# Indirect row writes of the last two chunks wait for the pair two back instead of the pair just in front

## The chip, the cores and the metric

The kernel is one program on one core of a Trainium2 chip, one launch. The metric is the device time of that core in microseconds (us). The engines are PE (TensorE, the matmul engine), DVE (VectorE), ACT (ScalarE), POOL (GpSimd) and SP (SyncE, which here only issues DMAs).

## What is computed

Two transformer layers over x of shape (16, 256, 128), 4096 tokens of 128 numbers, in float32. Around each half-layer stand a layer norm, a scale and a shift, and a gate. Layer 0 has causal attention and then a mixture of experts; layer 1 has a gated recurrence with a feed-forward block and then a channel mixer. The change lies in the mixture of experts of layer 0:

```python
def _L0_ffn_ref(x, gate_w, bias, up_w, up_b, down_w, down_b, sw_up, sb_up, sw_down, sb_down):
    scores = sigmoid(xf @ gate_w + bias)                      # 4096 tokens, 8 experts
    top_scores, top_idx = top_k(scores, 2)
    top_scores = top_scores / (sum(top_scores) + 1e-06)
    w = zeros((T, 8)).at[arange(T)[:, None], top_idx].add(top_scores)
    eo = gelu(up_w[e] @ x + up_b[e]) @ down_w[e] + down_b[e]  # for each expert e
    combined = einsum('teh,te->th', eo * 0.1, w)
    shared = (gelu(xf @ sw_up + sb_up) @ sw_down + sb_down) * 0.1
    out = shared + combined
    return out / (max(abs(out), axis=-1) + 1e-06)
```

Each token goes to two of the eight experts.

## The kernel before

The 4096 tokens are eight chunks of 512 (c = 0 to 7), two sequences each, and a chunk has four parts (k = 0 to 3) of 128 tokens. For each chunk the router's scores give, for every token, the two rows that it gets in the DRAM tensor `expert_rows` (`XD` in the code), where each expert has a region of its own; the row numbers stand in the tile IU (the function `dpd`, its last instruction is L1504). The chunk's tokens are transposed back into rows and copied by ACT into one of two tiles HT (`hta`, L1911; the profile calls the tile `five`). Then POOL writes them to DRAM: `scatter(c, k)` issues a pair of indirect DMAs (L2069), one for the first expert's row of each of the 128 tokens and one for the second's, 64 KB each. A pair counts on one of two semaphores, `scattered[k % 2]`, so parts 0 and 2 count on the first, parts 1 and 3 on the second; each pair adds 32, and a chunk adds 64 to each. Ahead of its pair each `scatter` waits for the pair just in front to have landed (L2067).

The experts work on tiles of 256 rows, 39 in all (the last ones have 128). The first 17 (N1) hold only rows of chunks 0 to 5 and can start before chunks 6 and 7 are written; every later tile waits for all eight chunks. For a tile t:

- `fetch(t)` on SP reads the expert's weights WE (L2187, 512 KB), the bias BD (L2188) and the tile's rows XT (L2191, 128 KB). It needs the output of tile t − 6 to be done, as there are six buffers, and from tile 17 on XT's read also waits for all scatters (L2190).
- `xt` on PE transposes XT (L1149), and `xs` on DVE copies the result to XS (L1648).
- `up` on PE, four parts of two matmuls (L1163), each followed by ACT's gelu into GF (L1923).
- `down` on PE, four parts of four matmuls (L1183), and `ev` on DVE, which adds the bias and writes the output tile YT (L1673).
- `store_rows` on POOL writes YT to `expert_rows` (L2082), in the place of the tile's input rows.

YT has three buffers, so `ev` of tile t waits for the store of tile t − 3 to have landed. XS has two.

Every engine runs its instructions in the order in which the program has them. That order is made by a planner (`schedule` and `arrange`) that walks a long written-out string of choices (ORDER1); it decides on which place of POOL's queue each scatter pair and each store stands. In the stretch around the change POOL's queue is: chunk 6 part 0; stores of tiles 0, 1, 2, 3; chunk 6 part 1; chunk 6 part 2; store 4; chunk 6 part 3; store 5; chunk 7 part 0; stores 6, 7; chunk 7 part 1; store 8; chunk 7 part 2; chunk 7 part 3; stores 9, 10, 11 and on. On DVE `ev` of tile 12 stands ahead of `xs` of tile 14, and on PE the order is: the last three quarters of `down` of tile 12 (twelve matmuls), three quarters of `up` of tile 13 (six), `xt` of tile 14, the rest of `up` of tile 13 (two), a quarter of `down` of tile 13 (four), and then half of `up` of tile 14 (four), and twelve of `down` of tile 13.

The two waits that matter, of `ev` (for u of at least 3) and of `fetch`:

```python
            if u >= 3:
                w.wait_ge(rows_out[u % 3], 16 * (u // 3))
```

```python
            w.for_all((landed, 64 * (NCH if t >= N1 else C1)) for landed in scattered)
```

`w.wait_ge` leaves a wait out where the same engine has already waited for that semaphore with at least that value.

Of the kernel before, what the change touches and what calls it, by code (L numbers as in the profile page):

```python
# [27 lines left out]
C1 = 6  # L28
# [687 lines left out]
def program(nc, i, out, ctx):  # L716
# [4 lines left out]
    def at(signal, *key):  # L721
        return sems[signal], P.nth[(SIGNALS[signal], *key)]

    def sem(name):
        return ctx.enter_context(nc.semaphore(name))
# [8 lines left out]
    scattered, rows_out, gathered = ([sem(f"{n}{k}") for k in range(m)] for n, m in (("scattered", 2), ("rows_out", 3), ("gathered", 2)))  # L734
# [1262 lines left out]
    def gpsimd(pool):  # L1997
        w = Waits(pool)
# [63 lines left out]
        def scatter(c, k):  # L2062
            w.wait_ge(*at("dp_ix", c))
            w.wait_ge(*at("ht", c))
            w.wait_ge(zero_rows, 16 * 17)
            if c or k:
                w.wait_ge(scattered[(k - 1) % 2], 64 * c + 32 * ((k + 1) // 2))  # L2067
            for n in range(2):
                pool.indirect_dma_start(out=XD[:, :], out_offset=bass.IndirectOffsetOnAxis(ap=IU[:, c, n, k:k + 1], axis=0),  # L2069
                                        in_=HT[c % 2][:, k, :], in_offset=None).then_inc(scattered[k % 2], 16)  # L2070
# [46 lines left out]
        def ux(c):  # L2117
# [3 lines left out]

        zero = pool.to_reg(0.0)
        do = {"ln_mod": ln_mod, "xlo": xlo_, "pjl": pjl, "kzp": kzp, "causal": causal, "scatter": scatter, "wsl": wsl, "store_rows": store_rows, "gather": gather,
              "hy": hy, "mix0": mix0, "ux": ux}
        for stage, *key in P.steps:
# [118 lines left out]
```

## Time and profile before

| | |
|---|---|
| Timed runs, median of 3 | 692.84 us (689.39 to 694.08) |
| Profiled execution: its own time | 686.2 us |
| Profiled execution: span of the trace | 684.6 us |
| Mean granted TensorE clock | 0.984 of full |
| PE busy | 641.7 us, 94% of the span |
| ACT, DVE, POOL busy | 479.7, 433.8, 394.3 us |
| Scatter instructions (L2069) | 64, 63.5 us in all; POOL idle before them 42.0 us, of it 21.0 for the landing of scatters |
| Output stores (L2082) | 39, 21.6 us in all; POOL idle before them 54.4 us |

"Busy" of an engine is a sum over the span, and idle time of an engine that no one waits for costs nothing. The rows of a timeline are instructions in order of start; in brackets stands how long the engine had been idle before and what ended it. PEclk is the granted clock of TensorE, 1.00 being 2.4 GHz and 0.50 being 1.2 GHz. Attention ends at about 290 us; the first expert tiles run from 300 us, beside the routing of chunks 6 and 7, and the chunks' scatters from 310 to 360 us.

### The profile page before, as it was taken

The page shows a single profiled execution, that of the slowest core. Times are in us where ns is not written, and L with a number is a line of the kernel's source. Part 1 is how long each engine was busy: PE and PEld are TensorE (multiplying, and loading weights), DVE is VectorE, ACT ScalarE, POOL GpSimd, SP SyncE. Part 2 cuts the span into 40 slices and gives each one's busy share as a digit, 9 for nine tenths or more (in the row PEclk, how much of TensorE's full clock was granted, in tenths as well). Part 3 has the DMA queues.
Part 4 walks back from the last instruction along what each step waited for, and adds up shares of the span by engine and source line. Part 5 has one row for each costly group of instructions (what it writes and reads, how often), then busy time and mean ns, then how long its engine had stood idle before and what let it go on. Part 6 is the DMA issues. An engine that isn't in the chain of part 4 may idle for free.

```text
span 684.6 us, 11622 instructions
## 1 busy us (share of the span) xinstructions
PE 641.7 (94%) x3699; PEld 437.7 (64%) x3699; DVE 433.8 (63%) x999; ACT 479.7 (70%) x763; POOL 394.3 (58%) x558
## 2 busy tenths in 40 slices
PE   7998999999998989999998999998989999999994
PEld 5565556655555646479887999976565664555642
DVE  3675676687879788653633644203668788777762
ACT  4866797887988777586443555643989887978563
POOL 5436377578878887813442455255677677725353
PEclk9998999999999999999999999999999999999998
DMA  9067750000000000068775587710111111000003
GB/s 247 4 237 281 261 215 9 21 11 19 18 21 15 26 26 20 28 197 266 250 250 181 178 250 246 215 43 27 34 31 30 31 28 28 12 0 16 16 1 93
DMA packets 46183, 66.45 MB, mean 97 GB/s; under 512 B 6753, under 2 KB 29114, under 8 KB 46122
## 3 DMA queue, kind: packets, MB, share of 16 engines
q1 hardware_dynamic: 39856, 52.62, 24.5%
q0 software_dynamic: 6208, 13.07, 5.9%
q8 instruction: 30, 0.49, 0.3%
q14 instruction: 31, 0.25, 0.1%
q10 hardware_dynamic: 58, 0.02, 0.0%
HBM read 37.31 MB, written 27.85 MB: 95 GB/s over the span
## 4 chain that ended last, share of the span: by engine, by line
PE 34%; POOL 10%; issue 9%; DVE 5%; DMA 4%; ACT 2%; POOLq 1%; SPq 1%; DVEq 0%; ACTq 0%
PE PS L1183 7%; POOL got L2097 4%; PE PS L1259 3%; PE PS L1163 2%; DMA got<-expert_rows,IU 2%; POOL H L2028 2%; PE PS L975 2%; PE PS L981 1%; PE PS L987 1%; PE PS L1170 1%; POOL xl L2034 1%; POOL expert_rows L2069 1%; PE PS L1171 1%; PE PS L1172 1%; PE PS L1083 1%
## 5 line engine op out<-in xcount | busy, mean ns | idle before, releaser
L1923 ACT ACTIVATE GF<-PS,XN 128x256 f32<-128x256 f32 (+1 forms) x156 | 68.3, 455 | 59.4 <-PE PS L1163 28.3
L2069 POOL DMA_INDIRECT expert_rows<-five,IU x64 | 63.5, 992 | 42.0 <-DMA expert_rows<-five,IU 21.0
L2097 POOL DMA_INDIRECT got<-expert_rows,IU x64 | 64.3, 1004 | 39.0 <-DMA got<-expert_rows,IU 21.7
L1183 PE MATMUL PS<-WE,GF 128*128 128x128 f32 x568 | 83.6, 277 | 1.4 <-ACT GF L1923 1.4
L1401 DVE TENSOR_REDUCE MX<-PS 128x4 f32<-128x896 f32 (+2 forms) x96 | 61.3, 685 | 27.3 <-PE PS L1046 27.0
L1183 PEld LDWEIGHTS PS<-WE,GF 128*128 128x128 f32 x568 | 75.5, 193 | 3.1 <-ACT GF L1923 2.0
L1884 ACT ACTIVATE PA<-PS 128x1024 f32<-128x1024 f32 x64 | 64.9, 1039 | 10.4 <-PE PS L1067 10.1
L2058 POOL TENSOR_SCALAR_AFFINE_SELECT PA<-PA 128x256 f32<-128x256 f32 x128 | 50.9, 427 | 13.6 <-ACT PA L1884 13.5
L2028 POOL TENSOR_SCALAR H<-xc,MOD 128x256 f32<-128x256 f32 x56 | 32.5, 588 | 39.0 <-DVE xc L1366 38.5
L2082 POOL DMA_DIRECT2D expert_rows<-YT x39 | 21.6, 555 | 54.4 <-issue 34.2
L1163 PE MATMUL PS<-XS,WE 128*128 128x256 f32 (+1 forms) x192 | 47.1, 357 | 4.6 <-DVE XS L1648 4.6
L1041 PE MATMUL PS<-KZ,QS 128*128 128x448 f32 (+2 forms) x192 | 47.7, 357 | 0.2
L2058 POOL TENSOR_SCALAR_AFFINE_SELECT PB<-PB 128x512 f32<-128x512 f32 x64 | 40.1, 652 | 12.4 <-ACT PB L1886 12.2
L1183 PEld LDWEIGHTS PS<-five,GF 128*128 128x128 f32 x256 | 32.9, 191 | 12.3 <-issue 11.0
L1041 PEld LDWEIGHTS PS<-KZ,QS 128*128 128x128 f32 x192 | 33.1, 199 | 6.1 <-issue 3.4
L1163 PEld LDWEIGHTS PS<-XS,WE 128*128 128x128 f32 x192 | 32.2, 194 | 7.1 <-DVE YT L1673 4.8
L1083 PE MATMUL PS<-PA,VA 128*32 128x512 f32 x256 | 35.6, 615 | 0.1
L975 PE MATMUL PS<-X,CT 128*128 128x512 f32 x64 | 34.1, 617 | 1.6 <-DVE X L1442 1.6
L1673 DVE TENSOR_TENSOR YT<-PS,BD 128x256 f32<-128x256 f32 (+1 forms) x39 | 15.5, 399 | 31.0 <-PE PS L1183 19.2
L1067 PE MATMUL PS<-QS,KZ 32*128 32x512 f32 x128 | 29.0, 505 | 6.0 <-DVE MX L1401 2.2
L1183 PE MATMUL PS<-five,GF 128*128 128x128 f32 x256 | 33.6, 275 | 0.0
L1886 ACT ACTIVATE PB<-PS 128x1024 f32<-128x1024 f32 x32 | 32.5, 1031 | 1.2 <-PE PS L1070 1.1
(337 smaller groups left out, 1748.2 us busy)
## 6 DMA issues: line engine op xcount, KB each, us to landing
WE<-in_experts SPq DMA_DIRECT2D x39, 512.0 KB
expert_rows<-five SPq DMA_DIRECT2D x16, 1024.0 KB, 9.0
XT<-expert_rows SPq DMA_DIRECT2D x32, 128.0 KB
expert_rows<-YT POOLq DMA_DIRECT2D x32, 128.0 KB
BD<-in_L_ffn_down_b SPq DMA_DIRECT2D x39, 64.0 KB
PA<-in_L_attn_x SPq DMA_DIRECT2D x8, 256.0 KB, 5.2
out<-yo SPq DMA_DIRECT2D x8, 256.0 KB, 2.4
expert_rows<-five,IU POOLq DMA_INDIRECT x64
```

Of the source, the lines that this page charges most:

```text
L975: pe.matmul(bank("lc", c, s), centre, chunk(X, c), start=True, stop=True).then_inc(sems["cen"], 1)
L1041: pe.matmul(pair("mxw", b, u)[:, a, o:o + 2 * n].rearrange("p (j n) -> p j n", j=2), q, kz[:, 2 * a:2 * a + 2, 0:n], start=True, stop=True)
L1083: m = pe.matmul(o, VA[:, 2 * b % 8, j, :], p0[:, j, 2 * h:2 * h + 2, :], start=True, stop=False)
L1163: pe.matmul(bk[:, 0:rows(u)], WU[u % NF][:, f], XS[slot["xs", u]][:, 0:rows(u)], start=True, stop=True).then_inc(sems["up"], 1)
L1183: m = pe.matmul(bk[:, b], g[:, b], wd[:, k, :], start=(k == 0 and t == 0), stop=(k == 3 and t == blocks - 1))
L1401: m = dve.tensor_reduce(mt[:, :, i].rearrange("p (a j) -> p a j", a=2), pair("mxw", b, u)[:, :, o:o + 2 * wd].rearrange("p a (j n) -> p a ...
L1884: m = act.activation(PT0[b % 2][:, j:j + 2, g:g + 2, :].rearrange("p j g n -> p j (g n)"), both, ACT.Exp, scale=SCALE)
L1923: act.activation(GF[slot["gf", kind, u, k]][:, 0:n], bank("up", kind, u, k)[:, 0:n], ACT.Gelu, bias=bias).then_inc(sems["gelu"], 1)
L2028: m = pool.tensor_scalar(hb(b), xc[:, S * n:S * n + S], mod(l, kc, b), mod(l, ks, b), ALU.mult, ALU.add)
L2058: m = pool.affine_select(out=a, in_=a, pattern=[[0, 2 if u < 4 else 4], [1, 128]], compare_op=ALU.is_ge, fill=zero, base=0, channel_multip ...
L2069: pool.indirect_dma_start(out=XD[:, :], out_offset=bass.IndirectOffsetOnAxis(ap=IU[:, c, n, k:k + 1], axis=0), in_=HT[c % 2][:, k, :], in_ ...
L2097: pool.indirect_dma_start(out=got[b][n][:, k, :], out_offset=None, in_=XD[:, :], in_offset=bass.IndirectOffsetOnAxis(ap=IU[:, c, n, k:k + ...
```

## The change

In `scatter`, for chunks 6 and 7 (c not below C1 = 6), the semaphore and the value that are waited for are others:

```diff
             if c or k:
-                w.wait_ge(scattered[(k - 1) % 2], 64 * c + 32 * ((k + 1) // 2))
+                w.wait_ge(scattered[(k - (c < C1)) % 2], 64 * c + 32 * ((k + (c < C1)) // 2))
             for n in range(2):
                 pool.indirect_dma_start(...)
```

For c below 6 the two lines say the same. For c of 6 and 7, part k now waits on `scattered[k % 2]` for 64c + 32(k // 2): parts 2 and 3 for parts 0 and 1 of the same chunk, parts 0 and 1 for parts 2 and 3 of the chunk before. Two pairs can so be under way at once, one on each semaphore. The order of the instructions is the same on every engine.

In POOL's queue (`expert_rows<-five,IU` are scatters, `expert_rows<-YT` stores) the stretch from chunk 6 part 1 to chunk 7 part 0 reads before:

```order
311 L2069 DMA expert_rows<-five,IU 33024x128 [waits scattered0]
312 L2069 DMA expert_rows<-five,IU 33024x128
313 L2069 DMA expert_rows<-five,IU 33024x128 [waits scattered1]
314 L2069 DMA expert_rows<-five,IU 33024x128
315 L2081 TENSOR_LOAD EI [waits s_ev]
316 L2081 ISA x2
317 L2082 ISA
318 L2082 DMA expert_rows<-YT 128x256
319 L2069 DMA expert_rows<-five,IU 33024x128 [waits scattered0]
320 L2069 DMA expert_rows<-five,IU 33024x128
```

and now:

```order
311 L2069 DMA expert_rows<-five,IU 33024x128 [waits scattered1]
312 L2069 DMA expert_rows<-five,IU 33024x128
313 L2069 DMA expert_rows<-five,IU 33024x128 [waits scattered0]
314 L2069 DMA expert_rows<-five,IU 33024x128
315 L2081 TENSOR_LOAD EI [waits s_ev]
316 L2081 ISA x2
317 L2082 ISA
318 L2082 DMA expert_rows<-YT 128x256
319 L2069 DMA expert_rows<-five,IU 33024x128 [waits scattered1]
320 L2069 DMA expert_rows<-five,IU 33024x128
```

Nothing moved; each pair names the other semaphore.

## Rows read from the trace of the kernel before

**Rows 1.** Waits of all engines, 318 to 364 us: who waited for whom, total, times, longest

```profile
POOL expert_rows L2069 <- DMA expert_rows<-five,IU: 16.8, 6, 4.5
...
PE PS L1163 <- DVE XS L1648: 4.6, 1, 4.6
```

**Rows 2.** Timeline of PE: start, duration, instruction, [idle before it <-releaser]

```profile
351.29 1.50 PE L1183 MATMUL PS<-WE,GF 128*128 128x128 f32 x12
...
353.50 0.61 PE L1183 MATMUL PS<-WE,GF 128*128 128x128 f32 x4
...
354.16 1.50 PE L1183 MATMUL PS<-WE,GF 128*128 128x128 f32 x12
...
356.80 0.38 PE L1149 MATMUL PS<-CT,XT 128*128 128x128 f32 x2
...
357.45 0.61 PE L1183 MATMUL PS<-WE,GF 128*128 128x128 f32 x4
362.69 2.05 PE L1163 MATMUL PS<-XS,WE 128*128 128x256 f32 x4 [4.64 <-DVE XS L1648]
...
366.58 0.60 PE L1163 MATMUL PS<-XS,WE 128*128 128x256 f32 x2
```

**Rows 3.** Timeline of DVE (YT is an expert tile's output, XS its input)

```profile
337.70 0.42 DVE L1673 TENSOR_TENSOR YT<-PS,BD 128x256 f32<-128x256 f32 x1 [1.07 <-DMA expert_rows<-YT]
...
342.57 0.41 DVE L1673 TENSOR_TENSOR YT<-PS,BD 128x256 f32<-128x256 f32 x1
...
346.85 0.42 DVE L1673 TENSOR_TENSOR YT<-PS,BD 128x256 f32<-128x256 f32 x1 [0.32 <-DMA expert_rows<-YT]
...
353.53 0.42 DVE L1673 TENSOR_TENSOR YT<-PS,BD 128x256 f32<-128x256 f32 x1 [3.36 <-DMA expert_rows<-YT]
...
361.79 0.42 DVE L1673 TENSOR_TENSOR YT<-PS,BD 128x256 f32<-128x256 f32 x1 [7.01 <-DMA expert_rows<-YT]
362.13 0.41 DVE L1648 COPY XS<-PS 128x256 f32<-128x256 f32 x1
```

**Rows 4.** Timeline of POOL (L2069 scatters, L2082 stores of output tiles)

```profile
325.38 0.99 POOL L2069 DMA_INDIRECT expert_rows<-five,IU  x1 [0.30 <-issue]
330.89 0.96 POOL L2069 DMA_INDIRECT expert_rows<-five,IU  x1 [4.52 <-DMA expert_rows<-five,IU]
...
335.51 0.99 POOL L2069 DMA_INDIRECT expert_rows<-five,IU  x1 [1.82 <-DMA expert_rows<-five,IU]
...
346.67 1.01 POOL L2069 DMA_INDIRECT expert_rows<-five,IU  x1 [3.02 <-DMA expert_rows<-five,IU]
...
348.99 0.58 POOL L2082 DMA_DIRECT2D expert_rows<-YT  x1
...
357.43 0.97 POOL L2069 DMA_INDIRECT expert_rows<-five,IU  x1 [4.28 <-DMA expert_rows<-five,IU]
...
359.67 1.69 POOL L2082 DMA_DIRECT2D expert_rows<-YT  x3
363.46 0.54 POOL L2082 DMA_DIRECT2D expert_rows<-YT  x1 [2.10 <-issue]
```

**Rows 5.** Windows of 1 us: busy time by engine, PEclk, DMA share, GB/s

```profile
363.00:364.00 1.00, 1.00 (x3) 0.82 (x3) 0.00 (x0) 0.01 (x1) 0.54 (x1) 0.50 0.10 26
```

**Rows 6.** Windows of 10 us, the same columns

```profile
350.00:360.00 10.00, 8.05 (x57) 7.40 (x55) 1.02 (x3) 4.38 (x11) 4.21 (x5) 1.00 0.74 229
360.00:370.00 10.00, 7.31 (x41) 6.77 (x42) 1.95 (x5) 1.89 (x4) 2.44 (x5) 0.83 0.53 154
370.00:380.00 10.00, 9.75 (x75) 9.04 (x73) 6.84 (x17) 5.59 (x12) 2.90 (x4) 1.00 0.70 248
```

**Rows 7.** Timeline of SP's DMA issues

```profile
355.33 0.33 SPq L2187 DMA_DIRECT2D WE<-in_experts  x1
...
361.16 0.33 SPq L2191 DMA_DIRECT2D XT<-expert_rows  x1
```

**Rows 8.** All scatter instructions of the run: duration ns min/median/max

```profile
L2069 POOL DMA_INDIRECT expert_rows<-five,IU x64: 963/982/1129, 115.1 to 358.7; - x64
```

## The prediction

> **What bounds the kernel now.** I read the page first. TensorE (PE) is busy 94% of the span, so a wait elsewhere counts only where it leaves PE without work. The change touches one kind of instruction, the scatter of token rows on POOL (L2069), for the last two of the eight chunks. Then I read the waits of the stretch in which those scatters run, 318 to 364 us. POOL stands 16.8 us in six waits, each for the landing of the pair of scatters just in front. PE's only large wait there is 4.6 us, for XS, an expert tile's transposed input that VectorE (DVE) copies out [rows 1]. The question is whether the second hangs on the first.
>
> The three timelines say yes. PE ends its work at 357.45 + 0.61 = 358.06 and starts again at 362.69 [rows 2]. DVE runs in order. It copies XS at 362.13, and right in front stands the output copy of tile 12 (YT, 361.79), for which DVE had been idle 7.01 us on a DMA that reads YT [rows 3]. YT has three buffers, so tile 12 needs the store of tile 9 to have landed. POOL issues that store at 359.67. Tile 9's output was complete at 346.85 + 0.42 = 347.27 [rows 3, 4]. It stood 12.4 us behind two scatter pairs, the second of which (chunk 7, part 3) had waited 4.28 us for the one in front [rows 4]. The chain is thus: scatter lands, next scatter, store 9, its landing, output 12, XS of tile 14, PE.
>
> PE also pays after the gap. PEclk is 0.50 in the window from 363, the lower of its two levels (1.2 GHz, after 4.6 us of idleness) [rows 5]. The four up and twelve down matmuls that start at 362.69 last until 366.58, 3.89 us. The same mix of shapes earlier took 353.50 − 351.29 = 2.21 us [rows 2]. The low clock costs 1.68 us.
>
> **The change part by part.** No instruction is added, removed or moved on any engine. Of the eight waits of these chunks, chunk 6 part 0 loses its wait for chunk 5 part 3, which changes nothing, since that pair landed long before; the other seven pairs wait for the pair two back. No wait is added.
>
> (a) POOL. A landing took at most 326.37 to 330.89, 4.52 us after the pair's end, for chunk 6 part 1 [rows 4]. The shortest is read at chunk 7 part 3: its issue ended at 359.67 and SP, which waits for all scatters before it reads tile 17, issued at 361.16, so 1.49 us [rows 4, 7]. I take the longest throughout. A pair takes 359.67 − 357.43 = 2.24 us of POOL, plus some 0.3 to get going. A store follows its output by 363.46 − (361.79 + 0.42) = 1.25 us [rows 3, 4].
>
> Chunk 6 part 2 starts behind part 1, at 326.7 in place of 330.89. Chunk 6 part 3 waits for part 1, so it starts where part 2 did before, 330.9, and ends at 333.2. It lands by 337.7. Chunk 7 part 1 needs that, and stands behind the store of tile 7. Output 7 ends at 338.12 (it waits 1.07 us for an older store now, which I keep), store 7 goes out at 339.4 and ends at 339.9, and chunk 7 part 1 runs from 340.2 to 342.5 in place of 346.67. The store of tile 8 follows output 8 (342.57 + 0.41), at 344.2, done at 344.8. Chunk 7 part 2 runs behind it to 347.4. Part 3 needs part 1 landed, 342.5 + 4.5 = 347.0, and runs 347.7 to 349.9. Store 9 follows at once, at 349.9 in place of 359.67, and ends at 350.5. With the 4.5 us of a slow landing it has landed at 355.0. The store of tile 8 took 349.57 to 353.53, 3.96 us, as output 11 shows [rows 3, 4].
>
> (b) DVE and PE. Output 12 now needs its own last products, the twelve that start at 354.16 and end at 355.66, and the store at 355.0. It runs at 355.7. The transpose for tile 14 ends at 356.80 + 0.38 = 357.18, XS is copied by 357.6, and PE needs it at 358.06 [rows 2, 3]. So nothing is late there, and the slack at DVE is about 1 us: output 12 may start as late as 356.8. The 4.64 us gap closes, and with it the clock's 1.68 us.
>
> (c) What is late next. Output 14 needs store 11. Its output now ends at 353.95 [rows 3], so the store goes out at 355.2 and has landed by 360.3, well before that output's products. The prefetch of tile 17, issued in part at 355.33 and stopped until 361.16 by the scatters, goes through undisturbed [rows 7]; tile 18 asks for its weights behind output 12, so some 6 us sooner. The DMA engines had 7.4 + 5.3 + 7.0 = 19.7 us of work between 350 and 380 [rows 6]. Squeezed into 23.7 us that is a share of 0.83, still below the whole. No fixed deadline stands behind this stretch, so what PE wins here the rest of the program should keep.
>
> Sum: 4.64 + 1.68 = 6.3 us off the profiled execution's 686.2, so 679.9. The bounds of the unknown, the landing of a scatter with another in flight, are the two ends above, 1.49 and 4.52 us. With 1.49 the sum is the same, as the gap is closed already. Beyond 4.52 no row goes; a gap begins again when landings reach about 5.5 us. On the median of the runs, 692.84, I take off the same amount: 686.5, 0.9% less. (About 1% is what a measurement of this kernel can tell from no change.)
>
> The profiled execution is 3.2 to 7.9 us shorter than the three timed ones. If that is slower DMA, each further microsecond of landing lengthened the old chain several times over, since it holds six such waits. This is a reason for a gain above 6.3 in the timed runs, and I give it a case below.
>
> One rule of the Trainium skill speaks against moving scatters. Row first: the 64 scatter instructions last 963 to 1129 ns, whatever DVE does beside them [rows 8]. The page "SBUF — State Buffer", section "SBUF: two separate sides", says that a DVE instruction in a two-port mode locks GpSimd out while it writes DMA descriptors, and that such a DMA went from about 620 to about 3100 ns. By that rule the scatters, now put where DVE works, would stretch by up to 2.5 us each and the sum would be nothing (rival E); by the row they stretch by 0.15 at most and the sum stays. I go with the row.
>
> **The rivals.**
>
> A, the time moves to another wait. PE runs on at 358 and soon meets something else: the weights of tile 15 or 16 not there, or the clock falling in another gap. For it: the DMA share rises to 0.83. Against: PE had no wait for a transfer in the stretch of rows 1, with the tiles fetched as far ahead as they will be, and DVE is idle most of the time (1.02 and 1.95 us busy of 10 in [rows 6]). Half the gap would come back: about 3 us gained, 689.8.
>
> B, the old chain is longer in the timed runs than in the profile. If half of the extra 3.2 to 7.9 us (2 to 4 us) lies in the six landings, the gain is 8.5 to 10 us: about 683.5. For it: the difference between profile and runs, and the spread of nearly 5 us among the three runs. Against: no row says where the extra lies.
>
> C, slower. Two pairs in flight share the DMA rings with the weight loads, and each landing doubles. With all landings L, store 9 has landed at 339 + 3L by the chain in (a) once L is over 6 (the third L is the store's own). Parity with the present 361.73 is at L = 7.6. 
>
> D, the change does nothing where it counts: the stores of tiles 6 to 8, not the landings, hold POOL. Against: outputs 8 and 9 were complete at 342.98 and 347.27, and their stores went out at 348.99 and 359.67, each behind a scatter pair that had waited 3.02 or 4.28 us for a landing [rows 3, 4]. Gain 1 us or less, 692.
>
> E, the scatter instructions themselves get longer where they now stand. Four of them lie between store 8 and store 9; if each took 2.5 us more, store 9 would go out at 349.9 + 10 = 359.9, as now, and the gain would be nothing: 692.8. Against: the range of rows 8, which allows 4 × 0.15 = 0.6 us, inside the slack. This is the case that the page above would make.
>
> **How the numbers follow.** Forecast (gap closed, 5.5 to 7.5 us gained) 0.55, A 0.13, B 0.22, C 0.05, D 0.03, E 0.02. The forecast's own spread touches the 1% line (6.93 us): I put 0.17 of its 0.55 above it. Faster by over 1%: 0.17 + 0.22 = 0.39, and 0.02 from chance differences, 0.41. Slower by over 1%: 0.03, from C and chance. Within 1%: 0.56. The range goes from a little beyond B (692.84 − 10, and 1.8 for chance, 681.0) to A and 1.2 for chance, 691.0.
>
> **What would show it.** Right: POOL's total wait for scatters falls from 16.8 to under 4 us; the pairs of chunks 6 and 7 end near 350 in place of 359.67; output 12 comes at about 356 with its releaser on PE; PE has no idle entry before tile 14's up matmuls; PEclk stays 1.00 between 360 and 370; the first matmuls of tile 17 come some 6 us sooner. Wrong: landings over 5.5 us, a PE gap near 358 that is only shorter, a new PE wait for XT or weights between 360 and 380, or all of this right and the end of the span moved by less, which would mean that a later stage gives it back.

## The result and the profile after

The changed kernel takes 682.95 us (median of 14 runs, 679.56 to 686.03); the kernel before, measured beside it, 690.7 us (14 runs, 687.08 to 694.67). The ratio is 0.990, 95% interval 0.9871 to 0.9928: 1.0% faster, or 6.9 us of 690.7, between 5.0 and 8.9 (the two medians by themselves are 7.75 us apart). The forecast was 6.3 us, 0.9%. The profiled execution takes 679.56 us with a span of 677.9, against 686.2 and 684.6.

The waits of the same stretch, after:

```profile
POOL expert_rows L2069 <- DMA expert_rows<-five,IU: 0.5, 1, 0.5
...
PE PS L1163 <- DVE XS L1648: 0.2, 1, 0.2
```

Against [rows 1], POOL's waits for scatters fell from 16.8 us in six to 0.5 in one, and PE's wait for XS from 4.6 to 0.2. The timeline of POOL after the change, from chunk 6 part 2 on (L2069 scatters, L2082 stores of output tiles; rows of three pairs and of store 9):

```profile
326.32 0.96 POOL L2069 DMA_INDIRECT expert_rows<-five,IU  x1 [0.30 <-issue]
...
339.95 1.02 POOL L2069 DMA_INDIRECT expert_rows<-five,IU  x1 [0.30 <-issue]
341.28 0.99 POOL L2069 DMA_INDIRECT expert_rows<-five,IU  x1 [0.30 <-issue]
...
347.31 0.96 POOL L2069 DMA_INDIRECT expert_rows<-five,IU  x1 [0.49 <-DMA expert_rows<-five,IU]
...
349.54 1.16 POOL L2082 DMA_DIRECT2D expert_rows<-YT  x2
```

Chunk 6 part 2 starts at 326.32 behind part 1, and the last pair starts at 347.31, where before it started at 357.43 [rows 4]. Store 9 goes out at 349.54 instead of 359.67. DVE and PE behind it:

```profile
352.23 0.42 DVE L1673 TENSOR_TENSOR YT<-PS,BD 128x256 f32<-128x256 f32 x1 [2.66 <-PE PS L1183]
...
355.10 0.42 DVE L1673 TENSOR_TENSOR YT<-PS,BD 128x256 f32<-128x256 f32 x1 [0.92 <-PE PS L1183]
356.61 0.42 DVE L1648 COPY XS<-PS 128x256 f32<-128x256 f32 x1 [1.09 <-PE PS L1149]
```

```profile
356.84 0.61 PE L1183 MATMUL PS<-WE,GF 128*128 128x128 f32 x4
357.29 1.03 PE L1163 MATMUL PS<-XS,WE 128*128 128x256 f32 x4
358.15 1.50 PE L1183 MATMUL PS<-WE,GF 128*128 128x128 f32 x12
359.49 0.60 PE L1163 MATMUL PS<-XS,WE 128*128 128x256 f32 x2
```

Output 12 (355.10) is now released by PE's own products and no longer by a DMA, and XS of tile 14 is copied at 356.61. PE goes from the record that starts at 356.84 straight into tile 14 at 357.29. From there to the next up are 359.49 − 357.29 = 2.20 us, against 3.89 in [rows 2]. The window in which PEclk had been 0.50 and the ones around it now read

```profile
355.00:375.00 20.00, 19.02 (x140) 17.75 (x139) 9.98 (x24) 10.04 (x22) 4.92 (x7) 1.00 0.78 241
```

PEclk 1.00 throughout.

Since two profiles of this program differ by more than the effect, I use one **stretch** that begins and ends inside the same trace: from the start of the first output store on POOL (L2082, 316.27 before, 315.91 after) to the start of the first matmul of L1201 behind the seventeenth tile on PE (376.73 and 369.64). The two ends are, before and then after:

```profile
316.27 0.60 POOL L2082 DMA_DIRECT2D expert_rows<-YT  x1 [3.56 <-issue]
...
376.73 1.47 PE L1201 MATMUL PS<-CT,gates 128*128 128x128 f32 x12
```

```profile
315.91 0.60 POOL L2082 DMA_DIRECT2D expert_rows<-YT  x1 [3.55 <-issue]
...
369.64 1.47 PE L1201 MATMUL PS<-CT,gates 128*128 128x128 f32 x12
```

The stretch was 60.46 us and is 53.73: 6.73 less. What follows the stretch took 307.87 and 308.26 us. So the whole gain was made here. The 0.39 us more behind it is within what that part differs by from run to run (307.5 to 308.8 us in all profiles but one), so nothing is seen to be given back.

### The profile page after: what moved, and what is told of

It is laid out like the page before. It is cut to its first block, busy times and chain, and to the rows that moved or that the text cites. A ratio compares the mean times of both kernels' runs of the same rounds, so it can differ in the third digit from the quotient of the medians.

```text
span 677.9 us, 11622 instructions
## 1 busy us (share of the span) xinstructions
PE 640.0 (94%) x3699; PEld 436.3 (64%) x3699; DVE 434.2 (64%) x999; ACT 480.4 (71%) x763; POOL 394.5 (58%) x558
## 4 chain that ended last, share of the span: by engine, by line
PE 43%; POOL 10%; DVE 8%; issue 6%; DMA 4%; ACT 3%; SPq 1%; POOLq 0%; DVEq 0%; ACTq 0%
PE PS L1183 9%; POOL got L2097 4%; PE PS L1163 4%; PE PS L1259 3%; DMA got<-expert_rows,IU 2%; PE PS L981 2%; POOL H L2028 2%; PE PS L975 2%; PE PS L1083 1%; PE PS L1041 1%; PE PS L987 1%; PE PS L1170 1%; PE PS L1171 1%; PE PS L1149 1%; POOL xl L2034 1%
## 5 line engine op out<-in xcount | busy, mean ns | idle before, releaser
L2069 POOL DMA_INDIRECT expert_rows<-five,IU x64 | 63.3, 989 | 26.3 <-issue 15.2
L2058 POOL TENSOR_SCALAR_AFFINE_SELECT PA<-PA 128x256 f32<-128x256 f32 x128 | 51.0, 428 | 13.5 <-ACT PA L1884 13.5
L2082 POOL DMA_DIRECT2D expert_rows<-YT x39 | 21.6, 555 | 62.8 <-issue 39.7
L1159 PE MATMUL PS<-H,five 128*128 128x512 f32 x64 | 31.8, 593 | 0.0
```

The costliest lines, as they stand in the source:

```text
L2058: m = pool.affine_select(out=a, in_=a, pattern=[[0, 2 if u < 4 else 4], [1, 128]], compare_op=ALU.is_ge, fill=zero, base=0, channel_multip ...
```

## The experiments

All ratios are to the kernel before, run beside it. "Stretch" is the one above. "Store 9" and "Output 12" are their starts on POOL and DVE, counted from the start of the stretch. In the expectations, times are those of the profile of before or after, as they say.

| Run | Stretch | Store 9 | Output 12 | PE gap at tile 14 | Ratio (95%) |
|---|---|---|---|---|---|
| before | 60.46 | 43.40 | 45.52 | 4.64 | 1 |
| the change | 53.73 | 33.63 | 39.19 | none | 0.990 (0.9871 to 0.9928) |
| e1 four YT buffers, old waits | 55.70 | 45.39 | 39.88 | none (1.65 at tile 15) | 0.9933 (0.9897 to 0.9968) |
| e2 chunk 7 only | 55.42 | 34.14 | 40.88 | none | 0.9923 (0.9878 to 0.9967) |
| e3 chunk 6 only | 62.31 | 44.33 | 46.45 | 4.66 | 1.0022 (0.9976 to 1.0067) |
| e4 unread matmuls, bank of output 12 | 64.24 | 43.09 | 45.21 | 4.25, ahead of them | one run |
| e5 unread matmuls, another bank | 58.34 | 42.33 | 45.02 | filled | one run |
| e6 last pair waits again | 54.75 | 37.23 | 41.43 | 0.79 | 0.9904 (0.9865 to 0.9942) |
| e7 XS ahead of output 12 | 60.97 | 43.79 | 45.91 | 4.93 | one run |
| e8 change and four YT buffers | 53.72 | 33.47 | 39.18 | none | 0.9902 (0.9871 to 0.9933) |
| e9 stores 9, 10 ahead, old waits | 53.73 | 37.52 | 40.41 | none | 0.9932 (0.9892 to 0.9972) |
| e10 all chunks | 53.71 | 33.44 | 39.17 | none | 0.9889 (0.9819 to 0.9959) |
| e11 before again | 61.08 | 43.28 | 45.41 | 4.93 | 1.0004 (0.9966 to 1.0043) |

The intervals of the ratios are about 0.4% wide on each side (0.7% for e10), so the times alone separate only groups: e3 and e11 from the rest. The stretch separates more.

**Four output buffers, the waits of before (e1).**

```diff
-    YT = [sb(f"YT{k}", [128, TR], where=moe) for k in range(3)]
+    YT = [sb(f"YT{k}", [128, TR], where=moe) for k in range(4)]
...
-            if u >= 3:
-                w.wait_ge(rows_out[u % 3], 16 * (u // 3))
+            if u >= 4:
+                w.wait_ge(rows_out[u % 4], 16 * (u // 4))
```

and four semaphores `rows_out` in place of three.

> The waits of before, but four YT buffers instead of three, so that the output of tile 12 needs store 8 (landed at 353.5 in the trace of before) and no longer store 9. Theory (the scatters hurt only through store 9 and the YT buffer): POOL still waits about 17 us for scatters and the last pair still ends near 360 us, yet PE has no gap near 358, PEclk stays 1.00 and the kernel is about 6 us (0.9%) faster than before; output 13 may wait about 2 us for store 9, and PE lose up to 0.5 us there. Rival (the late end of the scatters costs by itself, through the read of tile 17's rows that SP holds until 361, or through the DMA queue): the gap stays or comes back before 380, and the gain is under 2 us.

```profile
POOL expert_rows L2069 <- DMA expert_rows<-five,IU: 18.6, 6, 4.2
```

```profile
362.87 0.61 PE L1183 MATMUL PS<-WE,GF 128*128 128x128 f32 x4
363.31 1.03 PE L1163 MATMUL PS<-XS,WE 128*128 128x256 f32 x4
...
370.19 1.56 PE L1163 MATMUL PS<-XS,WE 128*128 128x256 f32 x6 [1.65 <-DVE XS L1648]
```

```profile
369.38 0.42 DVE L1673 TENSOR_TENSOR YT<-PS,BD 128x256 f32<-128x256 f32 x1 [6.33 <-DMA expert_rows<-YT]
369.73 0.41 DVE L1648 COPY XS<-PS 128x256 f32<-128x256 f32 x1
```

The waits view shows POOL waiting 18.6 us for scatters, more than before, and yet the gap at tile 14 is closed (362.87, then 363.31). So the buffer is a link of the chain, as the prediction had it. The gap is not gone but one tile further and smaller: output 13 (369.38) now waits 6.33 us for the landing of store 9, and PE stops 1.65 us at tile 15, where I had allowed 0.5. The late read of tile 17's rows cost nothing. The rival is out: the stretch is 4.8 us shorter with the last pair as late as ever, and the gap that is left hangs on store 9 and not on the scatters' end.

**Chunk 7 only (e2) and chunk 6 only (e3).** The condition `c < C1` of the change became `c < 7` and `c != 6`.

> Only chunk 7's four pairs wait for the pair two back; chunk 6 as before. By the chain: chunk 7 part 0 starts near 338.7, part 1 at 342.4, part 2 at 345.7, part 3 at 349.0 and ends at 351.3; store 9 has landed by about 356, in time for output 12. Theory: no PE gap, gain about 6 us, as with the whole change. Rival (all six removed waits add up): 16.8 us of waits fall to about 7 and the gain is a part of the whole, about 3 us.

> Only chunk 6's pairs wait for the pair two back; chunk 7 waits for the pair in front, as before. By the chain: chunk 7 part 0 starts near 338, 2 us sooner than before, but parts 1, 2 and 3 each wait for the landing in front (3.0, 1.3 and 4.3 us before), so store 9 goes out at 357 to 359. Theory: the PE gap shrinks from 4.6 us to between 2 and 4, the low clock behind it stays, gain 1 to 3 us. Rival (all six removed waits add up): two of six removed, gain about 2 us too; told apart from e2, which the theory puts at the whole and the rival at half.

The last pair of e3 on POOL, and PE behind it:

```profile
347.83 1.66 POOL L2069 DMA_INDIRECT expert_rows<-five,IU  x1 [3.21 <-DMA expert_rows<-five,IU]
...
354.78 0.99 POOL L2069 DMA_INDIRECT expert_rows<-five,IU  x1 [3.42 <-DMA expert_rows<-five,IU]
...
360.75 0.97 POOL L2069 DMA_INDIRECT expert_rows<-five,IU  x1 [3.71 <-DMA expert_rows<-five,IU]
...
362.99 1.69 POOL L2082 DMA_DIRECT2D expert_rows<-YT  x3
```

```profile
366.01 2.04 PE L1163 MATMUL PS<-XS,WE 128*128 128x256 f32 x4 [4.66 <-DVE XS L1648]
367.85 2.77 PE L1183 MATMUL PS<-WE,GF 128*128 128x128 f32 x12
```

Chunk 7 alone brings 5.0 of the stretch's 6.7 us, and the gap at tile 14 is gone (the record in front starts at 360.14, tile 14's first at 360.58); the rest is 1.4 us of earlier waits of PE for XS (0.47 and 0.89 us, tiles 11 and 12) and 0.2 more for a gelu, whose cause I did not settle. Chunk 6 alone brings nothing. The gap is 4.66 us as before, and the stretch 1.8 us longer than in the first profile of before, 1.2 than in the second. My step for e3 failed: I carried over the three waits of chunk 7 (3.0, 1.3, 4.3 us), but they were 3.21, 3.42 and 3.71 us now, and the last pair starts 42.1 us into the stretch instead of 41.2. The same bytes took other times to land once the pairs stood at other moments. That the weight loads beside them set this is likely but not shown: in the first profile the DMA share was 0.76 to 0.88 during the three landings of over 4.2 us and 0.37 during the shortest, but 0.93 during one of 2.4. The removed waits do not add up, in either direction.

The 1.8 us by which e3's stretch is longer have two halves. Output 12 starts 0.93 us later (46.45 against 45.52), and the records behind the gap take 0.93 us longer until the next transpose, as PEclk stayed at 0.50 until 371. A part of the first half is one scatter instruction, the 1.66 us at 347.83 above, where the other 831 of all thirteen profiles took 0.96 to 1.15. It starts while DVE is in this instruction:

```profile
347.12 1.46 DVE L1617 TENSOR_TENSOR XN<-XN,V 128x704 f32<-128x704 f32 x1
```

That is the sign that rival E of the prediction spoke of, at 0.7 us and not 2.5, and seen once. Whether DVE held the scatter was not tried.

**Unread matmuls in the gap, on two PSUM banks (e4, e5).** Both put 20 matmuls in front of tile 14's first up in the kernel before; nothing reads them.

```diff
+    n = P.count["fill"]
+    P.slot[("fill", n)], P.prior[("fill", n)] = P.slot[("up", "t", 14, 1)], P.prior[("up", "t", 14, 1)]
+    P.put("fill", n, 20)
+    P.steps.insert(P.steps.index(("up", "t", 14, 0)), P.steps.pop())
```

That is e5; e4 has `("up", "t", 14, 0)` in both places of the second line.

> Before, with 20 matmuls (128 columns, no one reads them) put in PE's queue ahead of tile 14's first up matmul, where the gap is: 20 x 0.215 = 4.3 us. The wait itself stays. Theory (the slow matmuls behind the gap are the clock's): PEclk stays 1.00, tile 14's four up and twelve down matmuls take 2.2 us from start to the next up instead of 3.9, and that part alone gains 1.7 us. Rival (they are slow for another reason, weights or gelu late): they still take over 3 us with PEclk 1.00.

> e4 again with the 20 unread matmuls on another PSUM bank: the one that tile 14's second up takes, which is free in time. In e4 they stood on the bank of its first up, and that bank is freed by output 12, so they started only behind the gap. Now they should run from about 358.1 (in the time of before) while XS is still missing. Theory (clock): PEclk stays 1.00 behind the gap, and from the first up of tile 14 to the first of tile 14's later ones 2.2 us pass instead of 3.9; 1.7 us of the 6.3 are the clock's. Rival (weights or gelu late behind the gap): still over 3 us.

e4 first, then e5, PE's timeline (L940 and L939 are the unread matmuls; the lines are shifted by 5 and 4):

```profile
361.60 0.61 PE L1188 MATMUL PS<-WE,GF 128*128 128x128 f32 x4
366.45 6.36 PE L940 MATMUL PS<-CT 128*128 128x128 f32 x40 [4.25 <-DVE YT L1678]
372.65 1.03 PE L1168 MATMUL PS<-XS,WE 128*128 128x256 f32 x4
```

```profile
359.47 0.61 PE L1187 MATMUL PS<-WE,GF 128*128 128x128 f32 x4
359.92 4.63 PE L939 MATMUL PS<-CT 128*128 128x128 f32 x40
364.50 1.10 PE L1167 MATMUL PS<-XS,WE 128*128 128x256 f32 x4
...
366.78 0.60 PE L1167 MATMUL PS<-XS,WE 128*128 128x256 f32 x2
```

In e4 the unread matmuls themselves waited 4.25 us, released by YT: they took the bank that output 12 has to free. PEclk fell while they ran (1.00 in the window from 366 us, 0.50 in those from 368 and 369, 1.00 again from 371), they took 6.2 us against 4.6 in e5, only lengthened the stretch, to 64.24 us, and left the question open. In e5 they ran at once. XS still came at 363.94, output 12 had waited 6.79 us, but the same four and twelve records now took 366.78 − 364.50 = 2.28 us instead of 3.89. The stretch is 58.34 us, 2.1 less than before, although nearly all of the wait is there: 0.5 of the 2.1 is that output 12 came sooner (45.02 against 45.52). So the clock's part is as the prediction had it, 1.6 us by the records. Each of the 20 matmuls has two records, and so has each up and down matmul of the expert tiles (the code issues four for an up and eight for a down, the trace has 8 and 16 records; a transpose, L1149, has one). So "four up and twelve down matmuls" in the prediction are two and six, and the numbers of up and down matmuls in the section on the kernel before are records, twice the matmuls. The sums of time do not change.

**XS ahead of output 12 on DVE (e7).**

```diff
+    P.steps.remove(("xs", 14))
+    P.steps.insert(P.steps.index(("ev", "t", 12)), ("xs", 14))
```

> Before, with the XS copy of tile 14 ahead of output 12 in DVE's queue. The prediction said that XS stood behind output 12; but tile 14's first up also takes the PSUM bank that output 12 reads. Theory now (two locks on one door): XS is copied by 357.7, yet PE still stops for 4.6 us at the same place, now released by YT, and the time is that of before. Rival (the prediction's step alone, DVE's order): the gap closes and tile 14 starts at 358.1.

```profile
359.03 0.42 DVE L1650 COPY XS<-PS 128x256 f32<-128x256 f32 x1 [2.43 <-PE PS L1151]
364.32 0.42 DVE L1675 TENSOR_TENSOR YT<-PS,BD 128x256 f32<-128x256 f32 x1 [4.87 <-DMA expert_rows<-YT]
```

```profile
359.26 0.61 PE L1185 MATMUL PS<-WE,GF 128*128 128x128 f32 x4
364.80 2.08 PE L1165 MATMUL PS<-XS,WE 128*128 128x256 f32 x4 [4.93 <-DVE YT L1675]
```

XS is ready at 359.45, and PE still stands 4.93 us, now with YT as the releaser. The stretch is 60.97 us, as before. Tile 14's first up takes the PSUM bank of tile 12's down products, and output 12 must read them first. Freeing XS is not enough.

**The last pair waits again (e6).** The condition became `c < C1 or (c, k) == (7, 3)`.

> The change as made, but the last pair (chunk 7 part 3) waits again for the pair just in front. Theory: one landing of 3.3 to 4.3 us comes back right ahead of store 9, which goes out at 353 to 354 instead of 349.5 (in the time of after) and lands near 357.5; output 12 runs near 358 and PE's gap before tile 14 is 1 to 2 us; gain 4 to 5 us (ratio about 0.993). Rival (the waits count by their total, which falls from 16.8 to about 4.5): gain three quarters of 6.3, the same size, but with no gap at tile 14.

```profile
355.93 0.97 POOL L2069 DMA_INDIRECT expert_rows<-five,IU  x1 [4.08 <-DMA expert_rows<-five,IU]
...
358.17 1.69 POOL L2082 DMA_DIRECT2D expert_rows<-YT  x3
```

```profile
361.87 0.61 PE L1183 MATMUL PS<-WE,GF 128*128 128x128 f32 x4
363.27 1.10 PE L1163 MATMUL PS<-XS,WE 128*128 128x256 f32 x4 [0.79 <-DVE XS L1648]
```

One landing of 4.08 us came back. Output 12 starts 2.24 us later in the stretch than after the change, PE stops for 0.79 us, and the stretch is 1.02 longer. The first 1.2 us of delay (2.24 − 1.02) cost nothing; the prediction had 1.1 of such slack. The gap was under my 1 to 2 us; the ratio does not tell it from the whole change.

**The stores of tiles 9 and 10 ahead of the last pair, the waits of before (e9).**

```diff
+    for t in (9, 10):
+        P.steps.remove(("store_rows", t))
+        P.steps.insert(P.steps.index(("scatter", 7, 3)), ("store_rows", t))
```

> The waits of before, but the stores of tiles 9 and 10 stand ahead of chunk 7 part 3 in POOL's queue. All six waits for the pair in front stay. Theory (what cost time was only that store 9 stood behind the wait of the last pair): store 9 goes out right behind part 2, near 353.2 in the time of before, and lands near 357.2; output 12 runs near 357.3, half a microsecond to one late; PE's gap shrinks from 4.6 us to under 1 and the clock holds; from the first output store to the 12 records of L1201 pass 55 us (60.5 before, 53.7 after); ratio 0.992 to 0.994. Rival (the waits themselves, or the late end of the scatters, cost): 60 us and a ratio of 1.

```profile
POOL expert_rows L2072 <- DMA expert_rows<-five,IU: 14.7, 6, 3.8
```

```profile
356.03 0.98 POOL L2072 DMA_INDIRECT expert_rows<-five,IU  x1 [2.61 <-DMA expert_rows<-five,IU]
...
358.28 1.15 POOL L2085 DMA_DIRECT2D expert_rows<-YT  x2
361.01 1.01 POOL L2072 DMA_INDIRECT expert_rows<-five,IU  x1 [1.57 <-DMA expert_rows<-five,IU]
```

```profile
361.55 0.61 PE L1186 MATMUL PS<-WE,GF 128*128 128x128 f32 x4
362.07 1.10 PE L1166 MATMUL PS<-XS,WE 128*128 128x256 f32 x4
```

This is the cleanest test. POOL still waits 14.7 us for scatters (L2072 is L2069 shifted), the last pair starts nearly as late as before in the stretch (40.3 us, 41.2 before), but stores 9 and 10 went out ahead of it. The stretch is 53.73 us, the same as with the change, and PE has no gap. I had expected up to 1 us of gap; store 9 landed in 2.3 us. What the six waits cost came through the place of stores 9 and 10 in POOL's queue.

**All chunks (e10), both remedies (e8), and before again (e11).** e10 has the condition `c < 0`; e8 is the change with e1's edit; e11 is the kernel before.

> Every chunk's pairs wait for the pair two back, not only those of chunks 6 and 7. In the trace of before chunks 0 to 5 have 4.2 us of such waits (21.0 less 16.8), none of them in front of something PE waits for. Theory: they go, the time is that of the change, ratio to before 0.990, the stretch from first output store to L1201 53.7 us. Rival (every removed wait counts): 3 us faster than the change.

> The change as made together with four YT buffers. Theory: the change alone has already taken all that this chain held, as its output stores land ahead of every output, so the ratio to before is that of the change, 0.990, and PE's waits between 318 and 400 are the same as after. Rival (the stores still cost somewhere after the change): over 2 us faster than the change alone.

> Before once more, nothing changed. It shows what the comparison makes of no change, and whether a second profile of the same program has the same stretch. Theory: ratio 1.000 within 0.4%; the stretch from first output store to L1201 again near 60.5 us with a PE gap of 4.6 us and PEclk 0.5 behind it, whatever the whole span is, since the spans of the other profiles differed ahead of that stretch (first store at 315.9 to 321.9 us). Rival (the timed runs are longer because landings are): where the span is longer, the stretch is longer.

The stretches of e8 and e10 are 53.72 and 53.71 us: nothing is left in this chain. Neither is shown to beat the change. That the waits of chunks 0 to 5 were free is not shown: they lie ahead of the stretch, where the profiles differ by more than those waits, and the ratio of e10 (four runs, 0.9819 to 0.9959) leaves room for the rival's 3 us. e11 has the gap (4.93 us) and a stretch of 61.08 us, 0.6 longer than I expected; its first store starts at 314.92, the earliest of all.

## Why the prediction was right

**The chain.** Scatter landing, next scatter, store 9, its landing, output 12, tile 14: right. e1 cut it at the buffer, e9 at the queue, e2 and e6 at the waits, and each closed the gap or nearly so, while e3, which left the waits ahead of store 9 in place, kept it whole.

**The last link** was told incompletely. I had XS alone as what holds PE, behind output 12 on DVE. There are two locks, XS and the PSUM bank, and both open with output 12 (e4, e7). For this change it made no difference. For a cheaper remedy, such as reordering DVE, it would have.

**POOL's new times (a).** Chunk 7 part 1 forecast 340.2, run 339.95; part 3 forecast 347.7, run 347.31; store 9 forecast 349.9, run 349.54. The whole trace was 0.36 us earlier, so these hold within 0.15 us. The landing of chunk 7 part 1 was longer than the 4.52 us that I had taken for the worst: from the end of its issue at 342.27 to 347.31 where part 3 starts, 5.0 us. It was the only wait left (0.49 us) and decided nothing.

**The sum.** 4.64 us of gap and 1.68 of clock. e5 measured the clock's part by itself, 3.89 − 2.28 = 1.6 us. The stretch lost 6.73 where the sum says 6.3. Of the 0.4 beyond, 0.25 lies ahead of the gap (the record in front of it starts 41.18 us into the stretch before and 40.93 after). PE's wait for a gelu near 334 us was 1.38 in the first profile and 0.94 or 0.95 in ten of the twelve others, that of before again (e11) among them, so this belongs to the execution and not to the change. The other 0.16 is in the gap: 4.64 is counted from the end of a record of 0.61 us, behind which the next one starts after 0.45 when nothing is late.

**The time itself** came out lower than forecast: 682.95 us against 686.5. Of these 3.5 us, 2.1 are that the kernel before has a median of 690.7 in 14 runs, where the prediction had three with 692.84. The other 1.4 are the difference of the medians, 7.75 instead of 6.3. That difference lies above the 5.5 to 7.5 of the forecast case, the 6.9 of the ratio inside it, so how near the size came is in part luck. The ratio of 0.990 lies on the 1% line, on whose two sides the prediction had put 0.56 and 0.41.

The size of the gain moves a little with the execution. In the second profile of before (e11) the gap was 4.93 us, and the four and twelve records behind it took 4.40 us instead of 3.89, as PEclk fell sooner and came back later (0.50 from 360 us on, while PE still stood, until 366; in the first profile from 363 to 366):

```profile
361.23 2.05 PE L1163 MATMUL PS<-XS,WE 128*128 128x256 f32 x4 [4.93 <-DVE XS L1648]
363.07 2.77 PE L1183 MATMUL PS<-WE,GF 128*128 128x128 f32 x12
365.63 0.82 PE L1163 MATMUL PS<-XS,WE 128*128 128x256 f32 x2
```

Gap and clock are 4.9 + 2.2 = 7.1 us there, and its stretch is 7.35 us longer than the change's. The whole difference between the two profiles of before is the clock's: output 12 starts at 45.41 and 45.52 us into the stretch. They put the gain at 6.7 and 7.4 us, the timed runs at 6.9.

**Rival B** (the timed runs are longer because of landings in this chain) is not borne out by the traces. The waits for landings in e11 are 16.6 us, as in the first profile. Where a stretch with the old waits was longer (e11 and e3), the clock made the whole or half of it. The timed gain, 5.0 to 8.9 us, does not exclude the lower end of B's 8.5 to 10, and no profile was taken of an execution of before as long as the slowest timed ones. Over all profiles the stretch's start lies anywhere from 314.9 to 321.9 us, with the same instructions ahead of it, and the rest behind it is 307.5 to 308.8 us in all but e11 (310.0). Most of the spread between executions is made ahead of the expert tiles.

**Rival A** (the time moves to another wait) did not happen for the change, but it is what e1 shows: a gap one tile on. **C** (doubled landings): one landing was 5.0 us, none near the 7.6 that parity needed; its reason, that the loads beside a landing set its length, stays unproven (see e3). **D** was out with POOL's first row. **E** (longer scatter instructions): the twelve that moved took 0.96 to 1.05 us; only e3 has a long one, of 1.66.

## What to carry to other kernels

On an engine that runs in order, a wait costs what stands behind it in its queue: look for the instruction behind the wait that someone else needs, and either shorten the wait, move that instruction ahead, or give its reader one more buffer. Here all three remedies took back most or all of the same gap, and the total of the waits said nothing about the gain (18.6 us of waits with most of the gain, 13.5 us with none of it). When the effect is smaller than the spread between executions, measure it inside a trace, between two landmarks on either side of the edit.

## What the runs showed of the hardware

A pair of indirect row writes (2 x 64 KB) landed in 1.5 to 5.0 us after its issue, always the same bytes; with two pairs in flight the landings that can be read took 5.0 us (the change), 4.9 (e8, e10) and 4.1 us (e6), and 1.5 to 4.9 with one (the longest in e4), so the runs do not show that a second pair lengthens them. Behind 4.6 to 4.9 us without work (before, e3, e7, e11) TensorE ran at the lower of its two levels and took 3.9 to 4.4 us for what else takes 2.2; behind gaps of 0.8 us (e6) and 1.65 us (e1) it kept the higher one. Kernels with the same instructions there differed by up to 7 us from one profiled execution to the next in the 315 us ahead of the stretch, and in the two compared here the granted clock (PEclk, the third number from the end) was different:

```profile
40.00:75.00 35.00, 31.94 (x208) 20.05 (x208) 20.94 (x54) 25.59 (x37) 18.92 (x37) 0.90 0.88 324
```

```profile
40.00:75.00 35.00, 33.06 (x199) 20.55 (x198) 21.02 (x54) 23.12 (x34) 16.46 (x32) 0.80 0.79 291
```

The first is before, the second e5, whose instructions are the same there: PEclk 0.90 and 0.80 between 40 and 75 us, and the first output store 2.3 us later in e5. What sets it was not tried.
